# Attention scores from two float32r halves, two heads at a time in the array's rows

## The reference

```python
q, k, v = (split_heads(x @ W + b) for W, b in ((Wq, bq), (Wk, bk), (Wv, bv)))
scores = jnp.einsum('bhqd,bhkd->bhqk', q, k) / jnp.sqrt(jnp.float32(dk))    # dk = 16
scores = jnp.where(causal[None, None], scores, -jnp.inf)
attn = jax.nn.softmax(scores, axis=-1)
out = jnp.einsum('bhqk,bhkd->bhqd', attn, v)
```

## Time and profile before

| | us |
|---|---|
| median of 3 runs | 1052.97 (1045.27 to 1053.01) |
| span of the profiled execution, first to last instruction | 975.7 |
| median less this span | 77.3 |
| attention stage, first scores to last turn of outputs | 118.61 to 605.71 |

### The profile page before, as it was taken

One profiled execution on the slowest core, in us unless ns is written; L12 is line 12 of the kernel. 1 busy time (PEld: TensorE's weight loads), 2 busy tenths in 40 slices (PEclk: granted clock), 3 DMA queues, 4 the chain that ended last, 5 costly groups with the idle time before them and its releaser, 6 DMA issues. The chain is left out here.

```text
span 975.7 us, 18404 instructions
## 1 busy us (share of the span) xinstructions
PE 854.0 (88%) x5476; PEld 478.9 (49%) x5477; DVE 660.1 (68%) x1527; ACT 476.2 (49%) x686; POOL 300.0 (31%) x368
## 2 busy tenths in 40 slices
PE   7979799999999989999999997799898999999300
PEld 4635434444444434444444432687556777777200
DVE  6428688888888887888888870489892122466364
ACT  3423266656666656656666566455322444444100
POOL 3423312211112111221112211442477500464373
PEclk9979899999999999999999999889899999999755
DMA  8773855444764266425754000710126745766443
GB/s 285 193 205 131 162 67 75 100 97 59 131 85 89 36 117 118 68 38 106 130 66 57 9 2 25 235 65 23 60 103 210 232 137 152 207 207 211 157 126 95
DMA packets 82464, 113.95 MB, mean 117 GB/s; under 512 B 8945, under 2 KB 60401, under 8 KB 82417
## 3 DMA queue, kind: packets, MB, share of 16 engines
q1 hardware_dynamic: 57808, 78.01, 38.1%
q0 software_dynamic: 6720, 18.88, 5.9%
q10 hardware_dynamic: 17888, 16.41, 5.2%
HBM read 62.55 MB, written 50.33 MB: 116 GB/s over the span
## 5 line engine op out<-in xcount | busy, mean ns | idle before, releaser
L658 ACT ACTIVATE work<-ps 128x1024 f32<-128x1024 f32 (+3 forms) x384 | 293.8, 811 | 185.5 <-PE ps L725 185.3
L335 DVE TENSOR_REDUCE m_neg<-ps 128x1 f32<-128x512 f32 (+3 forms) x432 | 265.6, 662 | 29.2 <-PE ps L320 18.7
L629 POOL TENSOR_SCALAR_AFFINE_SELECT work<-work 128x512 f32<-128x512 f32 x128 | 81.2, 634 | 394.4 <-ACT work L658 390.0
L317 PE MATMUL ps<-stacks 96*128 96x512 bf16 (+3 forms) x528 | 151.9, 332 | 1.5 <-DVE m_neg L335 1.5
L725 PE MATMUL ps<-stacks 99*128 99x512 bf16 (+3 forms) x528 | 124.6, 329 | 6.4 <-PEq L371 4.8
L335 DVE TENSOR_REDUCE m_neg_late<-ps 128x1 f32<-128x384 f32 (+3 forms) x176 | 106.7, 636 | 27.4 <-PE ps L320 27.4
L740 PE MATMUL ps<-work,vg 128*32 128x512 f32 (+3 forms) x1056 | 112.5, 498 | 1.6 <-POOL work L629 1.6
L320 PE MATMUL ps<-mask_b,ident_b 128*128 128x128 bf16 x512 | 100.3, 223 | 0.0
L317 PEld LDWEIGHTS ps<-stacks 96*128 96x128 bf16 x528 | 50.0, 98 | 95.0 <-DVE m_neg L335 48.8
L1243 DVE TENSOR_TENSOR work<-work,ps 128x256 f32<-128x256 f32 x48 | 20.2, 421 | 106.7 <-ACT work L1062 106.7
L1421 PE MATMUL ps<-wgu,work 128*128 x384 | 91.7, 382 | 0.3 <-issue 0.3
(11 more groups left out here) (143 smaller groups left out, 1098.4 us busy)
## 6 DMA issues: line engine op xcount, KB each, us to landing
stacks<-qk_parts SPq DMA_DIRECT2D x132, 128.0 KB, 6.3
qk_parts<-work SPq DMA_DIRECT2D x32, 384.0 KB, 3.0
y_sorted<-work SPq DMA_DIRECT2D x8, 1536.0 KB, 9.9
work<-y_sorted SPq DMA_DIRECT2D x48, 256.0 KB
z_sorted<-work ACTq DMA_DIRECT2D x48, 256.0 KB
wgu<-qk_parts SPq DMA_DIRECT2D x60, 128.0 KB, 6.5
work<-in_xT SPq DMA_DIRECT2D x8, 512.0 KB, 4.8
work<-in_x SPq DMA_DIRECT2D x8, 512.0 KB, 3.6
```

The costliest lines, as they stand in the source:

```text
L317: mm = pe.matmul(dst, qs[r][0:KS, h0 + m, qt * P:(qt + 1) * P], ks[r][0:KS, h0 + m, half * CH:half * CH + w], start=True, stop=not diag)
L335: dve.tensor_reduce(dst, ps[:, bank, 0:heads * w].rearrange("p (h k) -> p h k", h=heads), AX.X, ALU.max, negate=True).then_inc(reduced, 1)
L629: pool.affine_select(out=blk_, in_=blk_, compare_op=ALU.is_ge, fill=0.0, base=0, pattern=[[0, GH], [1, P]], channel_multiplier=-1).then_in ...
L658: act.activation(probs[:, s + 2 * pair:s + 2 * pair + 2, off:CH], ps[:, SCORE_BANK + 2 * pair:SCORE_BANK + 2 * pair + 2, off:CH], ACT.Exp, ...
```

## The change

- q and k are written as two float32r parts: ACT rounds the high part, DVE writes the rest as the low part. ACT's second rounding and POOL's subtraction go. Stores grow from 3 x 2 to 2 x 4 bytes an element.
- Three products instead of six: 48 rows and two for the maximum (50). Two heads lie one under the other, at rows 0 and 64 of the stacks, and their matmuls go to rows 0 to 63 and 64 to 127 of the array, into two banks. `load_stacks` issues 18 DMAs a step for the same bytes, `load_max` four for three.
- A piece holds two heads in two banks: 21 pieces a step. The mask is added by four matmuls of 64 rows a pair of heads, two of them only 64 columns wide, from two constants with their halves exchanged.
- Scores and pieces share one ring of three slots of two banks (banks 0 to 5). Turned maxima and outputs share bank 7.
- The maxima's split into two parts moves to POOL; only the minimum of their two halves stays on DVE. One float32 transpose turns the maxima of a half.
- `early` uses one slot (banks 6 and 7) and waits for the item before, not for the one before that.
- The stacks (now 3 of their own) no longer share memory with the experts' weights.

```diff
-PRODUCTS = [(0, 0), (0, 1), (1, 0), (0, 2), (2, 0), (1, 1)]
+PRODUCTS = [(0, 0), (0, 1), (1, 0)]
 KS = len(PRODUCTS) * DK
-KM = KS + 3
+KM = KS + 2
+ROWS = 64
+PAIRED = GH // 2
+LOADS = 16 * len(PRODUCTS) * 2 * (PAIRED + 1)
...
-        heads = 4 if w == P else 2 if w == 2 * P else 1
-        MAXES += [(qt, h, heads, half, w) for h in range(0, GH, heads)]
+        heads = 2 if w <= 2 * P and qt != NT - 3 else 1
+        MAXES += [(qt, h, heads, half, w) for h in range(0, PAIRED, heads)]
...
-RING = [4, 5, 7]
+SLOTS = 3
+OUT_BANK, TURN_BANK = 6, 7
...
-    cost = [unit_width(u) * (2 if what == "weigh" else 1) for what, u, _ in main]
-    pieces = [m[2] * m[4] + 60 for m in MAXES]
+    cost = [0 if what == "weigh" else 2 * unit_width(u) + 230 for what, u, _ in main]
+    pieces = [2 * m[2] * m[4] + 140 for m in MAXES]
...
+RING_USERS = [item for item in ORDER if item[0] in ("scores", "max")]
+TURNS = [item for item in ORDER if item[0] in ("turn_max", "turn_out")]
+assert len(RING_USERS) % SLOTS == 0
+def slot_bank(item):
+    return 2 * (RING_USERS.index(item) % SLOTS)
...
+def slot_before(item, first, last):
+    at = RING_USERS.index(item) - SLOTS
     while at >= 0:
         if present(RING_USERS[at], first, last):
             return RING_USERS[at], 0
-        at -= len(RING)
+        at -= SLOTS
     if first:
         return None, 0
-    at += len(RING_USERS)
-    while not present(RING_USERS[at], second, False):
-        at -= len(RING)
-    return RING_USERS[at], 1
+    return RING_USERS[at + len(RING_USERS)], 1
...
-EARLY_BANKS = [6, 7]
+EARLY_BANK = 6
...
-        qk_parts = dram("qk_parts", (2, 3, B * D, N), BF16)
+        qk_parts = dram("qk_parts", (2, 2, B * D, N), F32)
...
         def load_stacks(sp, i, r):
             for n, (qp, kp) in enumerate(PRODUCTS):
...
+                q_rows, k_rows = [qk_parts[s, part, bass.ds(i * GW, GW), :]
+                                  .rearrange("(a x d) t -> x d a t", a=PAIRED, d=DK)
+                                  for s, part in ((0, qp), (1, kp))]
+                for x in range(2):
+                    rows = slice(x * ROWS + n * DK, x * ROWS + (n + 1) * DK)
+                    for a in range(PAIRED):
+                        sp.dma_start(qs[r][rows, :, a].bitcast(F32),
+                                     q_rows[x][:, a].rearrange("d (c t) -> d c t", c=HALVES))\
+                            .then_inc(stack_loaded[r], 16)
+                    sp.dma_start(ks[r][rows].bitcast(F32), k_rows[x]).then_inc(stack_loaded[r], 16)
...
+            qt, p0, pairs, half, w = MAXES[n]
+            diag = half == qt // CT
+            for m in range(pairs):
+                dst = [ps[:, bank + x, m * w:(m + 1) * w] for x in range(2)]
+                for x in range(2):
+                    rows = slice(x * ROWS, x * ROWS + KS)
+                    mm = pe.matmul(dst[x], qs[r][rows, qt // CT, p0 + m, qt % CT * P:(qt % CT + 1) * P],
+                                   ks[r][rows, p0 + m, half * CH:half * CH + w], start=True, stop=not diag)
                 if diag:
-                    mm = pe.matmul(dst[:, w - P:w], ident_b[:, :], mask_b[:, :], start=False, stop=True)
+                    for j in range(2):
+                        for x in range(2):
+                            rows = slice(x * ROWS, (x + 1) * ROWS)
+                            one, low = (ident_b, mask_b) if j == x else (ident_x, mask_x)
+                            mm = pe.matmul(dst[x][:, w - P + j * ROWS:w], one[rows, :], low[rows, j * ROWS:P],
+                                           start=False, stop=j == 1)
             mm.then_inc(score_max_ready, 1)
...
+            pe.transpose(ps[:, bank, 0:P], m_parts[:, qc].bitcast(F32), ident[:, :]).then_inc(mT_ready[qc], 1)
...
+            dst = (m_neg[:, qt // CT] if half == 0 else m_late)[:, :, p0:p0 + pairs, qt % CT]
+            if n in (0, NM0):
+                wait_count(dve, m_ready[qt // CT], i)
             dve.wait_ge(score_max_ready, NM * i + n + 1)
-            dve.tensor_reduce(dst, ps[:, bank, 0:heads * w].rearrange("p (h k) -> p h k", h=heads), AX.X, ALU.max,
-                              negate=True).then_inc(reduced, 1)
+            dve.tensor_reduce(dst, ps[:, bank:bank + 2, 0:pairs * w].rearrange("p x (a k) -> p x a k", a=pairs), AX.X,
+                              ALU.max, negate=True).then_inc(reduced, 1)
...
+            dve.tensor_copy(mT[qc][:, :], ps[0:2 * GH * CT, bank, 0:P]).then_inc(mT_copied[qc], 1)
...
+        def both_halves(dve, i):
+            dve.wait_ge(reduced, NM * i + NM)
+            dve.tensor_tensor(m_neg[:, 1], m_neg[:, 1], m_late[:, :, :, :], ALU.min).then_inc(m_both, 1)
+        def max_parts(pool, i, qc):
+            high = m_parts[:, qc, 0:GH * CT]
+            low = m_parts[:, qc, GH * CT:2 * GH * CT]
+            m = m_neg[:, qc].rearrange("p x a t -> p (x a t)")
+            done = 2 * i + qc
+            wait_apart(pool, *((m_both, i + 1) if qc else (reduced, NM * i + NM0)), pool_waited)
+            if not (isinstance(i, int) and i == 0):
+                wait_apart(pool, mT_ready[qc], i, pool_waited)
+            pool.tensor_copy(high, m).then_inc(m_step, 1)
+            pool.wait_ge(m_step, done + 1)
+            pool.tensor_tensor(low, m, high.bitcast(F32), ALU.subtract).then_inc(m_ready[qc], 1)
...
         def load_max(sp, i, r, qc):
             sp.wait_ge(mT_copied[qc], i + 1)
-            for part in range(3):
-                sp.dma_start(qs[r][KS + part:KS + part + 1, :, qc * CH:(qc + 1) * CH],
-                             mT[qc][part * GH:(part + 1) * GH, :]).then_inc(m_loaded[qc], 16)
+            for part in range(2):
+                for x in range(2):
+                    row = x * ROWS + KS + part
+                    at = (part * 2 + x) * PAIRED * CT
+                    sp.dma_start(qs[r][row:row + 1, qc].bitcast(F32).rearrange("o a n -> o (a n)")
+                                 .rearrange("o (b q) -> o b q", q=P),
+                                 mT[qc][at:at + PAIRED * CT, :]).then_inc(m_loaded[qc], 16)
...
-                    dve.memset(ks[r][KS:KM], 1.0).then_inc(ones_ready, 1)
+                    for x in range(2):
+                        dve.memset(ks[r][x * ROWS + 32:(x + 1) * ROWS].bitcast(F32), 1.0).then_inc(stack_ones, 1)
...
+                        dve.scalar_tensor_tensor(parts[t][:, 1, :], ps[:, t, :], bqk[:, t // 2, t % 2:t % 2 + 1],
+                                                 parts[t][:, 0, :].bitcast(F32), ALU.add, ALU.subtract)\
+                            .then_inc(low_ready[t], 1)
...
-                        if k >= 2:
-                            what, n = EARLY[k - 2]
+                            pe.wait_ge(halves_loaded, 16 * HALF_CONSTANTS)
+                            pe.wait_ge(stack_loaded[0], LOADS)
+                        if k >= 1:
+                            what, n = EARLY[k - 1]
...
+                    max_parts(pool, i, 1)
...
+                        max_parts(pool, i + 1, 0)
...
+                def scores(i, r, u, pair, first, last):
                     qc, kt = UNITS[u]
                     off = CH - unit_width(u)
+                    bank = slot_bank(("scores", u, pair))
                     if pair == 0 and kt == 0:
-                        pe.wait_ge(m_loaded[qc], 48 * i + 48)
-                    wait_count(pe, exp_done, 2 * (NU * i + u) + pair - 1)
-                    for h in (2 * pair, 2 * pair + 1):
-                        mm = pe.matmul(ps[:, SCORE_BANK + h, off:CH], ks[r][0:KM, h, kt * P:(kt + 1) * P],
-                                       qs[r][0:KM, h, qc * CH + off:(qc + 1) * CH], start=True, stop=True)
+                        pe.wait_ge(m_loaded[qc], 64 * i + 64)
+                    slot_free(i, ("scores", u, pair), first, last)
+                    for x in range(2):
+                        rows = slice(x * ROWS, x * ROWS + KM)
+                        mm = pe.matmul(ps[:, bank + x, off:CH], ks[r][rows, pair, kt * P:(kt + 1) * P],
+                                       qs[r][rows, qc, pair, off:CH], start=True, stop=True)
                     mm.then_inc(score_ready, 1)
...
+                def slot_free(i, item, first, last):
+                    before, ago = slot_before(item, first, last)
+                    if before is None:
+                        return
+                    what, n, pair = before
+                    if what == "max":
+                        wait_count(pe, reduced, NM * (i + 1 - ago) + n + 1)
+                    else:
+                        wait_count(pe, exp_done, 2 * (NU * (i - ago) + n) + pair + 1)
```

More of the change, by code:

```diff
@@ L8 @@
 BF16 = mybir.dt.bfloat16
+F32R = mybir.dt.float32r
 I32 = mybir.dt.int32
@@ L15 @@
 CONSTANTS = 6
+HALF_CONSTANTS = 4
 P = 128
@@ L107, in present @@
     return not (first and item == ("turn_out", 1, 0))
-def ring_before(item, first, last, second=False):
-    at = RING_USERS.index(item) - len(RING)
+def slot_before(item, first, last):
```

(47 more changed lines are left out.)

154 lines of the change are left out of this document (57 added, 97 removed).

## The result

The changed kernel takes 1078.63 us (median of four runs, 1074.74 to 1086.37), the kernel before 1051.84 (1045.27 to 1053.01) on the same chip: ratio 1.0293, 95% interval 1.0235 to 1.0351. It is slower by 3%, where 1048 and a small gain were forecast. The time lies inside the range, but the forecast is wrong in its sign. A kernel's executions differ by some per cent at times, and a ratio is taken from the quicker ones of both kernels, so it needn't be the quotient of the two medians.

What follows compares the result with a forecast made beforehand. PE's queue was taken to bound attention steps, with waits for ring slots next. Fifteen steps at -0.51 (-7.7), last step -0.4 and start +3 gave -5: 1052.97 to 1048 us, range 1028 to 1110.

Steps and rivals of the forecast that it cites:

- rival 4: PE's clock in attention falls to 1.2 GHz throughout, a step taking 41.7 us: +177, so 1230 us; chance 0.05.
- 29.85 us a step: One attention step, walked in written order: 29.63 plus 0.2, so 0.5 us below now.
- The unit by hand: One full-width unit of an attention step, from scores through exponential and refill to weighing: 2.94 us, about 0.7 idle.
- rival 2: Both weight loads of a scores pair go one after the other, 0.20 behind each wait: +19, 1072 us; chance 0.11.
- rival 1: Cheap turns (0.17) and loads behind waits (0.05) in attention: step 28.35 + 0.2, -25, 1028 us; chance 0.17.
- rival 3: Scores pairs do not run together, or stream at the f32 rate: +57, 1110 us, up to 1125; chance 0.17.
- The loads, POOL and the maxima: In an attention step: DVE 22.9 us, ACT 19.2, POOL below 8; four maxima DMAs take 2.5, without stall.
- The ring: Scores and maxima share three slots in attention; most of the 8 us PE saves turns into waiting for slots.
- The start: Before attention: early items +6, halved streams give back 3.4, memsets about +0.5; sum +3 us, from 0 to +7.
- Last step -0.4: Attention's last step gets 0.4 us faster, being bound by exponentials already.
- PE busy below 26: Sign that the forecast is right: PE busy for less than 26 us in an attention step.
- The median of the runs lies 77.3 us above the span: Whole kernel: timed runs take 77.3 us more than the profiled span, a part taken as unchanged.

Runs made afterwards that it cites:

- experiment 2: The changed kernel run again unchanged, against the kernel before: 1019.54 us, ratio 1.0297 (1.0139 to 1.0455).
- experiment 11: The changed kernel, still looped, with the second half of each maxima mask left out, against the kernel before: 1006.61 us, ratio 1.0302.
- experiment 12: The changed kernel with the second half of each maxima mask left out and PE's loop written out, against the kernel before: 1070.61 us, ratio 1.0224.
- experiment 7: The changed kernel with PE's loop written out and both matmuls of a scores pair in the same rows, against the kernel before: 1245.77 us, ratio 1.2527.
- experiment 3: The changed kernel with PE's loop over the attention steps written out, against the kernel before: 988.31 us, ratio 1.0082.
- experiment 6: The kernel before with PE's loop over the attention steps written out, against the kernel before: 972.61 us, ratio 0.9918.
- experiment 1: The kernel before, unchanged, with a profile of its own: 980.2 us, ratio 1.0021.
- experiment 10: The kernel before with each mask matmul of the maxima issued twice, against the kernel before: 1009.9 us, ratio 1.0317.

## Why the prediction was wrong, step by step

**The failed steps.** The first is missing: the sum has terms for the steps, the start and the last step, and none for the jumps of PE's loop, though the profile of before has one gap of 2.87 us behind a jump and the change adds 26 matmuls to a step (5892 - 5476 on the pages, over 16 steps). That is three gaps instead of one. The second is rival 4's "With about 25 of 30 and waits of 0.3 to 0.8 I expect it to hold." The clock holds in an undisturbed step (27.8 busy of 30.6), but after a gap it stays low for 10 to 31 us, and with 32 mask matmuls a step fewer it falls by itself. The shown profile of after also has two such falls (10.2 us each, at 170 and 235 us) ahead of its first gap; that of experiment 2, the same kernel, has none. Rival 4 had only the case "throughout", 1230, and no part of it. The Trainium skill (TensorE: Matmul & The Clock Gate, "psum-queue depth-cycling") says that a PE which cycles through PSUM banks and micro-idles between groups swings between the two clocks; experiments 11 and 12 agree, with falls of 10.2 us and no wait over 0.7 ahead of them. That such waits are needed for a low clock isn't so: in experiment 7 it stayed low for 114 us without any.

**Size of the terms, on chips of the quicker kind.** Jumps with the clock behind them: 31 us in the changed kernel, 7 in the one before, +24. The rest, 16 us, is what experiments 3 and 6 differ by; their traces, 13.0 apart in span, put 13.9 at: start +2.2, fourteen steps +6.6 (of which 14 x 0.3 = 4.2 at the full clock, the rest the cold clock of the first), last two +5.1.

**"29.85 us a step"**: 30.6. The term that was left out is the weight load of a scores pair right behind a weighing or a transpose: the prediction put a load of 0.10 behind waits and let all others hide. The unit by hand was 2.94, "0.22+0.17+0.04+1.03+0.04+0.10+0.22+1.12" in short. In the timeline of experiment 3 it is 3.05 (326.78 to 329.83): until ACT starts 0.55, not 0.43, which is the load; the exponential 1.03; 0.04; the piece and the weighing together 1.43 (0.44 and 0.99), not 1.44. The price for a load behind a wait was right, and rival 2 is out: its sign, "0.11 apart behind each wait", isn't there (both loads in 0.19, where the same rows take 0.29). The 14 pairs behind a weighing or a transpose, at 0.10 each, are an estimate of at most 1.4 us a step; not all of them are waited for, and steps came out 0.75 longer than forecast. How that is spread over the units isn't shown. The Trainium skill (TensorE: Matmul & The Clock Gate, "Why this matters for your kernels") has tiles in different rows start within 4 ns of each other; the trace agrees for these float32r pairs, behind a wait too, with 3 to 4 ns.

**Luck.** The 1078.63 lies inside the range of 1028 to 1110, which was drawn from rival 1 to rival 3, and close to rival 2's 1072. None of the mechanisms of rivals 1 to 3 is in the trace, so that the time fell inside was luck.

**Right.** The pair runs together: 0.50 against 0.73 in the same rows, so rival 3 is out. The loads, POOL and the maxima: DVE 23.62 (22.9 forecast), ACT 20.04 (19.2), POOL 6.44 (below 8); four maxima DMAs issue in 2.81 us (2.5), and no wait of PE on them is in the profile of after. The ring is the next bound: PE's idle time in steps is ended by L683 and L366, as named. The start: attention begins at 120.92 instead of 118.61, +2.3 (+3.8 and +2.2 in the experiments), forecast +3; the wait at its start is 3.61 (4.84).

**Wrong, and small.** "Last step -0.4": the last two steps cost +5. Without maxima beside it PE waits 2.14 and 1.29 us for exponentials (the last row of stretches above: 20.91 busy of 28.31), and the clock is 0.88 there, not 1.00. "PE busy below 26" was no fair sign: a record reaches until its result can be read, so many short matmuls with waits between them still add up to 27.9.

**"The median of the runs lies 77.3 us above the span; that part is unchanged."** Nothing lies around the span but 1.8 us (1086.37 against 1084.6) or 2.0 (978.25 against 976.2 in experiment 1). The shown profile came from an execution whose last stage is 70 us shorter than in the timed ones. As the change doesn't touch that stage this moved the forecast by nothing, but the reading was wrong.

## What to carry to other kernels

Before adding instructions to an engine's loop, look at its jumps: an "issue" gap at one of them in the profile, and the count of instruction packets, tell that the body may be near the size that is still kept; written out, or with fewer and longer passes, the loop loses the gap. Work taken from PE that turns into waits can be paid twice, once as waiting and once when the clock falls (experiments 11 and 12), so change the order of the fills together with the change that shortens them: here that order and the loop written out turned +3% into -2.8%. With f32 weights, price one load at every pair behind a wait, a weighing or a transpose; for two matmuls in different rows it is one load, not two.

## What the hardware showed that was not expected

- A jump of PE's loop costs 2.5 to 4.8 us where the pass is loaded again, and then 3.4 us (experiment 10) to 31 us (experiment 2) at 1.2 GHz. Written out, the same instructions are loaded without a gap.
- The clock isn't a matter of idle time alone: with scores matmuls in rows 0 to 63 only, one after the other, it stayed at 1.2 GHz for 114 us with PE busy for 114.00, while the same kernel with pairs in both row halves (experiment 3) held 2.4 GHz at 27.8 of 30.6.
- Two f32 weight loads for different rows go side by side, both in 0.19 us; for the same rows they take 0.29 (experiment 7).
